# A one-core transformer block on Trainium2: image 3's row maxima moved behind image 1's second variance on VectorE

## The reference

```
x = x + conv_ref(ln_c(x))                       # attention, per image:
    q = wq·xf + bq ; k = wk·xf + bk ; v = wv·xf + bv
    attn = softmax(q · k) ; out = v · attnᵀ
t = tokens(x)
t = t + ffn_ref(ln_t(t))                        # per token:
    weights = softmax(xt @ Wr + br), the top 2 of 8, scaled to sum 1
    xn = (xt - mean) * rsqrt(var + 1e-5)
    y_e = gelu((xn * g_e + b_e) @ W1_e + b1_e) @ W2_e + b2_e
    out = sum over the two experts of weight * y_e
```

## Time and profile before

| what | value |
|---|---|
| time, three runs | 56.33, 56.64, 56.64 us (median 56.64) |
| the profiled execution | 56.28 us, span of the instructions 54.5 us |
| TensorE busy | 49.7 us (91% of the span) |
| VectorE busy | 37.5 us (69%) |
| ScalarE busy | 32.0 us (59%) |
| GpSimd busy | 18.8 us (35%) |
| chain of waits, by engine | TensorE 83%, VectorE 8%, issue 2% |

### The profile page before, as it was taken

The page is one execution under the profiler, slowest core; times in us unless marked ns, Lnnn a source line. Parts: engine busy times, 40 slices in busy tenths (PEclk is TensorE's granted clock), DMA queues, the critical chain, the costliest instruction groups (busy, mean ns, idle before and its releaser), DMA issues.

```text
span 54.5 us, 2448 instructions
## 1 busy us (share of the span) xinstructions
PE 49.7 (91%) x976; PEld 36.8 (67%) x976; DVE 37.5 (69%) x171; ACT 32.0 (59%) x75; POOL 18.8 (35%) x44
## 2 busy tenths in 40 slices
PE   4999979999968899999999999999999999999900
PEld 2332646976746795597577799896758997599800
DVE  3098689699999795999626899839910319748920
ACT  4600386993796959994499990100699701994000
POOL 4129588000055499996529990000000000000000
DMA  0351366967000000000000000000011000000022
GB/s 0 96 127 19 78 144 137 375 222 268 12 6 0 6 0 0 12 0 0 0 0 18 0 0 12 0 0 12 0 48 48 12 0 0 12 0 6 12 48 48
DMA packets 2940, 2.42 MB, mean 44 GB/s; under 512 B 2032, under 2 KB 2544, under 8 KB 2928
## 3 DMA queue, kind: packets, MB, share of 16 engines
q1 hardware_dynamic: 2608, 2.23, 13.5%
q10 hardware_dynamic: 320, 0.03, 0.5%
HBM read 2.00 MB, written 0.26 MB: 41 GB/s over the span
## 4 chain that ended last, share of the span: by engine, by line
PE 83%; DVE 8%; issue 2%; ACT 1%; DVEq 0%; ACTq 0%
PE banks L960 24%; PE banks L996 22%; PE banks L820 9%; PE banks L1014 7%; PE banks L858 4%; PE banks L937 3%; PE banks L837 3%; PE banks L887 2%; PE banks L902 2%; PE banks L866 2%; PE banks L828 2%; PE banks L845 2%; DVE nmax L529 1%; PE banks L977 1%; DVE res L706 1%
## 5 line engine op out<-in xcount | busy, mean ns | idle before, releaser
L431 ACT ACTIVATE H<-banks,PF 128x512 f32<-128x512 f32 x32 | 19.3, 708 | 7.8 <-PE banks L960 7.3
L960 PE MATMUL banks<-XE,W1F 64*64 64x256 f32 x224 | 13.7, 382 | 0.0
L996 PEld LDWEIGHTS banks<-W2F,H 128*64 128x64 f32 x384 | 11.6, 138 | 1.3 <-issue 1.2
L996 PE MATMUL banks<-W2F,H 128*64 128x64 f32 x384 | 12.2, 223 | 0.0
L960 PEld LDWEIGHTS banks<-XE,W1F 64*64 64x64 f32 x224 | 7.9, 133 | 3.4 <-issue 0.6
L321 POOL TENSOR_SCALAR XE<-XF,PF,LB 128x256 f32<-128x256 f32 x14 | 7.8, 567 | 1.6 <-ACT XF L409 1.6
L820 PE MATMUL banks<-const-bfloat16-1.0 128*128 128x512 bf16 x11 | 4.9, 615 | 0.8 <-PEq L1124 0.8
L299 POOL TENSOR_TENSOR rs<-base,half 128x2 f32<-128x2 f32 x4 | 2.8, 701 | 6.9 <-DVE base L570 6.8
L392 ACT ACTIVATE PR<-banks,nmax 128x256 f32<-128x256 f32 x8 | 3.8, 481 | 1.3 <-DVE nmax L529 1.2
L658 DVE TENSOR_TENSOR prod<-banks,gate 128x512 f32<-128x512 f32 x4 | 2.8, 690 | 2.3 <-PE banks L996 2.3
L1014 PEld LDWEIGHTS banks<-W2F,H 128*64 128x64 f32 x128 | 3.9, 138 | 0.5 <-issue 0.4
(11 more groups left out here) (81 smaller groups left out, 69.4 us busy)
## 6 DMA issues: line engine op xcount, KB each, us to landing
W1F<-in_w_dram SPq DMA_DIRECT2D x1, 768.0 KB, 4.5
W2F<-in_w_dram SPq DMA_DIRECT2D x1, 512.0 KB, 4.7
W1F<-in_w_dram SPq DMA_DIRECT2D x1, 256.0 KB, 3.4
X<-in_x_dram SPq DMA_DIRECT2D x2, 64.0 KB, 1.9
X<-in_x_dram SPq DMA_DIRECT2D x1, 128.0 KB, 2.3
B2D<-in_b_dram SPq DMA_DIRECT2D x8, 2.0 KB
out_dram<-res SPq DMA_DIRECT2D x1, 128.0 KB, 1.7
out_dram<-res SPq DMA_DIRECT2D x2, 64.0 KB, 1.8
```

The costliest lines, as they stand in the source:

```text
L431: nc.scalar.activation(H[:, r, :].rearrange("p (t n) -> p t n", t=PT), ps_z[z_slot(g // J)][:, :, PIX * j:PIX * j + PIX], ACT.Gelu, bias=P ...
L960: mm = nc.tensor.matmul(ps_z[z_slot(q)][C * c:C * c + C, k, PIX * j:PIX * j + PIX], W1F[rows, e, j, C * c:C * c + C], XE[h][rows, e, :], s ...
L996: mm = nc.tensor.matmul(ps_y[s % 2][C * c:C * c + C, k, n, :], H[:, (2 * J * s + J * k + j) % RING, left:left + C], W2F[:, J * (2 * p + k) ...
```

## The change

On VectorE, `peaks(3)` goes from behind `second_stats(0)` to behind `second_variance(1)`, and `second_variance(0)` goes from behind `sum_tokens(1)` to ahead of it. No instruction is added, removed or changed in size, and the other engines' lists are the same.

```
             sum_tokens(0)
             peaks(2)
             second_stats(0)
-            peaks(3)
             second_moments(0)
+            second_variance(0)
             sum_tokens(1)
-            second_variance(0)
             second_stats(1)
             second_moments(1)
             second_variance(1)
+            peaks(3)
             second_norm(0)
             probs(2, 1)
             second_norm(1)
```

## The result

The changed kernel takes 59.19 us (median of five runs, 59.07 to 59.66) where the kernel before, run beside it, takes 56.33 us (56.03 to 56.64). The ratio is 1.053, with a 95% interval of 1.048 to 1.058. So the change is slower, as forecast, but by 2.9 us and not by 1.7. The profiled execution took 59.66 us, 3.38 more than the one before.

A forecast was written before the change was run, and what follows sets the result against it. The prediction took a solid block of TensorE matmuls from 18.10 us as the bound, its late start delaying the end. Profiled 56.28 us plus 1.78 shift gave 58.06; 0.24 for run levels made 58.3 us, range 57.8 to 59.1.

The forecast's parts named there:

- The shift: Image 3's exponentials on ScalarE start 1.96 us later; TensorE regains 0.18, so image 1's turned residual comes 1.78 us later.
- The room of 0.25 us on ScalarE: Image 3's maximum is ready 0.25 us before ScalarE begins its exponentials, so it could be that much later.
- The variance: On VectorE, moving image 0's variance ahead of image 1's residual gains 0 us, with bounds of 0 and 0.18.
- The clock: Rival: TensorE's 2.4 us gap drops its clock to half speed, costing up to 2.2 us, up to 60.5; chance 0.10.
- Part lost later: Rival: slack behind 18.1 us absorbs some delay, or the maximum runs sooner; 0.6 to 1.3 us slower, chance 0.04.
- not slower: Rival: the delay is hidden altogether and image 0's earlier norm starts TensorE's matmul block sooner; 56.2 to 56.6 us, chance 0.02.

The follow-up runs named there:

- experiment 6: The changed kernel with image 3's maximum moved up to right behind image 0's second variance, ahead of image 1's residual: 56.57 us, ratio 1.007.
- experiment 3: The kernel before with only image 0's variance moved ahead of image 1's residual, image 3's maximum left in place: 56.51 us, ratio 1.004.
- experiment 2: The kernel before with only image 3's maximum moved behind image 1's second variance: 59.31 us, ratio 1.051.
- experiment 1: The changed kernel with ten constant matmuls filling TensorE's gap ahead of image 3's transposes: 57.78 us, ratio 1.028.

## Why the prediction was partly wrong

**The shift (forecast 1.78 us): the mechanism was right and the size close.** The start of image 1's residual (14.96 less the opening), the start of the maximum (16.28 against 16.31), the delay of the exponentials (1.92 us against 1.96) and the queues behind them came as worked out. The turned residual of image 0 follows the transposes after 0.49 us, and I had 0.58. The room of 0.25 us on ScalarE is nearer 0.2 (experiment 6). In the filled kernel, where nothing else disturbs it, the shift is 1.66 us at image 1's turned residual and 1.50 us between medians.

**The variance (forecast 0): right** as a part of this change. Alone it costs up to 0.2 us (experiment 3).

**The clock: the step that failed.** The sum has no term for it, and I gave 0.10 to the case that the gap of 2.4 us puts TensorE's clock down, on the ground that gaps of 0.21 and 0.42 us brought no slower matmul and that the gap stands behind 15 us of nearly unbroken work. Neither ground bears on a gap five times as long, and the second is refuted for this gap: the same work stood ahead of it and the clock fell in 5 of 5 runs. That costs 1.64 us in the profiled execution and 1.4 between medians. This rival was the case that came; its bound of 2.2 us took 4.42 us at half speed, and the low stretch lasted 3.41 us. The clock didn't fall where I had it, either: in the profiled execution image 3's transposes, the first turned residual and image 2's attention matmuls still ran at full speed, and the fall came 2 us behind the gap's end. The range ended at 59.1, 0.09 below the median, because I had let only a short low stretch into it.

The trace before held no gap long enough to decide it, and there the rule of the Trainium skill, "TensorE: Matmul & The Clock Gate", section "HAM oscillation — how this bites in real kernels", pointed the right way: a long enough wait between bursts of matmuls brings the lower clock back, and the next burst starts at it. This case's traces agree that the clock falls (0.50 from 20.5 to 23.5 us), and they show that the burst need not start low.

**"Part lost later" and "not slower"** didn't occur: from 23.8 us on TensorE is busy without a pause as before, and gives back only 0.19 us.

## What to carry to other kernels

Before a step is moved back, ask how much room its consumer has, and then count what stands behind the consumer in its own queue: here 0.2 us of room on ScalarE, and the whole rest of the kernel behind it. If the move opens a gap on TensorE, price the gap twice, once as delay and once as half speed for a stretch of the work that follows, and take the second as likely, not as a tail, once the gap is several times longer than any that the trace shows at full clock (here 2.3 us against 0.42). Here, filling the gap with constant matmuls into a free bank won the second price back (59.2 to 57.8 us), but not the first; two matmuls of the ten were not enough.

## What the runs showed that I had not expected

- TensorE's clock can fall after gaps of 1.4 to 1.8 us, and it does so in some runs and not in others of the same kernel (1 of 6 and 5 of 6).
- The fall can come 2 us behind the end of the gap (20.2 against 18.25 us), during solid work, or inside the gap (experiment 2). It came 13.65 us behind the rise in the opening in all five traces that have it.
- The low stretch lasts 3.41 us in four of these traces and 6.83 in experiment 2; the matmuls in it take up to twice as long (the first layer 3.54 us in place of 1.90).
- The opening matmuls run at about half rate at first (a start every 0.43 us for 512 columns, and one every 0.22 in experiment 1's filler), while the granted clock of that stretch is given as 1.00, since the records of the clock begin with its rise. At the start of an execution the durations tell the clock and that column doesn't.
